# A four-layer kernel on one core: where the next batch's keys stand among a batch's queries, and a second expert product that leaves its result transposed

## The reference, cut to what matters

```python
x = ln(x + linear_attention(x))      # (4, 2048, 256): per head phi = (exp(x orf / d^.25 - norm) + 1e-6) / sqrt(m)
                                     #   kv = sum over l of phi_k v;  out = phi_q kv / (phi_q ksum), then Wo, bo
x = ln(x + fp4_ffn(x))               # gate, up, down with blockwise FP4 values of inputs and weights
x = ln(x + softmax_attention(x))     # 16 heads, rope over the head axis, 2048 x 2048 per head
# experts: 2 groups of 4096 rows, 8 experts, 160 slots each, the best 2 experts of a row
gate, idx = top_k(softmax(x @ w_router), 2)
pos = cumsum(mask) - 1               # a row's slot in its expert; slots >= 160 are dropped
h = relu(einsum('egch,ehf->egcf', expert_in, wi))       # 160 x 256 -> 160 x 1024 per expert
expert_out = einsum('egcf,efh->egch', h, wo)            # -> 160 x 256
x = ln(x + combine(expert_out, gate))
```

## Time and profile before

| | |
|---|---|
| median of 3 runs | 4830.02 us (4827.56 to 4838.83) |
| the profiled execution's own time | 4828.89 us |
| its span in the profile | 4827.1 us |
| PE busy | 4518.8 us, 94% of the span |
| DVE, ACT, POOL busy | 3535.6, 2783.8, 1025.5 us |
| queries with the next keys, three batches | 98.25 to 727.00 us |
| after the third layer's last product | 4545 to 4827.1 us |

### The profile page before, as it was taken

How to read it: one execution, slowest core, us unless ns; L and a number is a source line. 1 busy time by engine, 2 the same in 40 slices (tenths; PEclk the granted TensorE clock), 3 DMA queues, 4 the chain that set the end, 5 groups by cost and what they waited for, 6 DMA issues and landing times. The chain is left out here.

```text
span 4827.1 us, 65506 instructions
## 1 busy us (share of the span) xinstructions
PE 4518.8 (94%) x25453; PEld 1687.8 (35%) x25456; DVE 3535.6 (73%) x3881; ACT 2783.8 (58%) x5253; POOL 1025.5 (21%) x991
## 2 busy tenths in 40 slices
PE   8988888999997999999999999999999999999895
PEld 4434343666662222222222222222222232222374
DVE  2554446887787777898777888777888988898141
ACT  2222222333332777888777777777777767788511
POOL 2333325344431121000121110112111011000223
PEclk9999999999997999999999999999999999999998
DMA  3000100011211333212333222223222121122323
GB/s 101 29 20 23 57 9 19 9 46 46 83 49 56 110 102 101 63 47 70 101 101 116 66 77 73 83 96 127 63 81 80 52 71 60 70 72 74 105 93 58
DMA packets 233083, 333.24 MB, mean 69 GB/s; under 512 B 37026, under 2 KB 174308, under 8 KB 230724
## 3 DMA queue, kind: packets, MB, share of 16 engines
q1 hardware_dynamic: 229892, 321.19, 20.3%
q0 software_dynamic: 2880, 7.87, 0.9%
HBM read 221.50 MB, written 98.04 MB: 66 GB/s over the span
## 5 line engine op out<-in xcount | busy, mean ns | idle before, releaser
L1555 DVE TENSOR_REDUCE mx<-ps 128x1 f32<-128x1024 f32 x2048 | 2405.8, 1218 | 434.3 <-PE ps L717 431.7
L1307 ACT ACTIVATE Pb<-ps 128x512 f32<-128x512 f32 x4096 | 2201.7, 597 | 498.1 <-PE ps L717 493.8
L717 PE MATMUL ps<-QS,KS 98*128 98x512 bf16 x4096 | 1250.4, 386 | 16.7 <-ACT Pb L1307 5.4
L717 PE MATMUL ps<-Pb,VA 128*32 128x512 f32 x8192 | 1097.9, 608 | 0.1
L717 PE MATMUL ps<-KM,QM 64*128 64x512 bf16 x4096 | 661.0, 390 | 58.0 <-DVE mx L1555 55.9
L717 PEld LDWEIGHTS ps<-QS,KS 98*128 98x128 bf16 x4096 | 261.6, 98 | 1082.6 <-ACT Pb L1307 884.5
L717 PEld LDWEIGHTS ps<-KM,QM 64*128 64x128 bf16 x4096 | 179.4, 93 | 614.3 <-issue 347.8
L1877 POOL CAST mrow<-mres 16x128 bf16<-16x128 f32 x64 | 18.0, 280 | 1347.5 <-ACT mres L1137 1347.5
L717 PEld LDWEIGHTS ps<-Pb,VA 128*32 128x32 f32 x8192 | 161.4, 108 | 399.9 <-issue 398.9
L717 PE MATMUL ps<-wdT,hT 128*128 128x256 f32 (+1 forms) x768 | 195.3, 397 | 19.7 <-DVE X L1540 14.8
L1154 ACT ACTIVATE phi<-phi 128x1024 f32<-128x1024 f32 x64 | 67.6, 1057 | 223.6 <-DVE phi L1429 223.6
(11 more groups left out here) (250 smaller groups left out, 4517.8 us busy)
## 6 DMA issues: line engine op xcount, KB each, us to landing
QM<-qd SPq DMA_DIRECT2D x128, 256.0 KB
KM<-kd SPq DMA_DIRECT2D x128, 256.0 KB
qd<-parts SPq DMA_DIRECT2D x96, 256.0 KB, 2.8
kd<-parts SPq DMA_DIRECT2D x96, 256.0 KB, 2.8
QS<-qd SPq DMA_DIRECT2D x64, 384.0 KB
KS<-kd SPq DMA_DIRECT2D x64, 384.0 KB
vdr<-vst SPq DMA_DIRECT2D x64, 256.0 KB, 2.7
den<-rd SPq DMA_DIRECT2D x64, 256.0 KB
```

What stands on the lines that cost most here:

```text
L717: return eng.matmul(out, a, b, start=start, stop=stop, skip_group_check=skip)
L1307: eng.activation(Pb[(u - 1) % 9], o, ACT.Exp, bias=0.0, scale=0.25).then_inc(act_A, 1)
L1555: eng.tensor_reduce(mx4[qc % 2][:, 4 * i + q, h:h + 1], o, AX, ALU.max).then_inc(dve_D, 1)
```

## The change

- `woven` and the two rates go. `beside_queries` issues each step of the queries, then one step of the weights, then a fixed number of key steps: 2 behind the second `q`, 2 behind `nq`, 1 behind the second `pq` of each half, 2 behind the second `num`, 1 behind the second `o`, and none elsewhere; 9 a chunk, 36 a batch.
- `kv` lags `phi` by two tiles in place of one (one more step at the end of a batch's keys: 36).
- In n = 15 the output stages are issued at `OUT_LAST`; the finish of tiles 48 and later has one blank step in place of three, and two `fo` in one step; `oa` of the last quarter is issued ahead of the background work that is left; `second` is rearranged.
- `ed` takes `wo` as weights (128 x 128) and 160 columns of `h`: the result is transposed, 128 x 320 for both halves. ACT copies it to `yT` (4 experts' room), the new `yt` transposes it back by blocks of 128 slots (PE in bank 5, ACT to one of 6 `er` buffers, SP stores it to `eo`), and `yw` takes the own results from `er` block by block: `yo` and its loads go. `eu` has three banks in place of four.

```diff
 OUT = {0: ("oa",), 5: ("ob", "oc"), 7: ("od",), 10: ("oe",), 12: ("og",)}
-KRATE = 46
-WRATE = 45
+
...
+            yield [("phi", n)] + [("kv", n - 2)] * (n % 16 > 1)
             if ahead:
                 yield ahead[j:j + 1] if j < 3 else ahead[3:]
         if b == 0:
             yield [("rl", 2 * C), ("rl", 2 * C + 1)]
+    yield [("kv", 16 * b + 14)]
     yield [("kv", 16 * b + 15), ("kvs", b)]
...
 
+def beside_queries(plan, b, keys, weights):
+
+    behind = {"q": (0, 2), "nq": (2,), "pq": (0, 1, 0, 1), "num": (0, 2), "o": (0, 1)}
+    for units in queries_order(b, range(4), 0):
+        plan += units + next(weights, [])
+        for name, C in (u[:2] for u in units if u[0] in behind):
+            at = sum(u[:2] == (name, C) for u in plan)
+            for _ in range(behind[name][at - 1]):
+                plan += next(keys, [])
+
+
 def weights_order():
...
-            yield []
-        for j in range(4):
-            yield [("fo", T0 + j)]
+        yield from [[]] * (1 if T0 >= 48 else 3)
+
+        for j in range(0, 4, 2):
+            if T0 >= 48:
+                yield [("fo", T0 + j), ("fo", T0 + j + 1)]
+            else:
+                yield [("fo", T0 + j)]
+                yield [("fo", T0 + j + 1)]
         yield [("st2", T0)]
         yield []
         yield [("ap2", T0)]
...
+
+    came = lambda e: range((160 * e + 127) // 128, (160 * (e + 1) + 127) // 128)
+    done = lambda e: range(160 * e // 128, 160 * (e + 1) // 128)
+
+    def back(e):
+        yield from ([("yt", g, b), ("yw", g, b)] for b in done(e))
+
+    yield from ([("xt", g, b)] for b in came(0))
     for e in range(8):
-        for n in range(3):
-            yield [("eu", g, e, n)]
+        yield [("eu", g, e, 0)]
+        if e > 1:
+            yield from back(e - 2)
+        yield [("eu", g, e, 1)]
+        yield [("eu", g, e, 2)]
         if e < 7:
-            for b in range((160 * (e + 1) + 127) // 128, (160 * (e + 2) + 127) // 128):
-                yield [("xt", g, b)]
+            yield from ([("xt", g, b)] for b in came(e + 1))
         if e:
             yield [("ed", g, e - 1)]
+    yield from back(6)
     yield [("ed", g, 7)]
+    yield from back(7)
 
 
 def final_order(g):
-    yield [("yo", g, 0), ("yo", g, 1)] if g else [("yo", g, 0)]
-    yield [("yw", g, 0), ("gp", g, 0)]
     if g == 0:
-        yield [("yp", g, 0)]
-        yield [("yo", g, 1), ("yn", g, 0), ("ys", g, 0)]
-        yield [("yw", g, 1), ("gp", g, 1)]
-        yield [("yp", g, 1)]
-        yield [("yn", g, 1), ("ys", g, 1)]
+        for f in range(2):
+            yield []
+            yield [("gp", g, f)]
+            yield []
...
-    while True:
-        k = min(range(len(streams)), key=lambda n: at[n])
-        at[k] += 1.0 / streams[k][1]
-        units = next(streams[k][0], None)
-        if units is not None:
-            plan += units
-        elif k == 0:
-            return
 
 
 def make_plan():
...
         k = keys_order(b + 1)
-        woven(plan, (queries_order(b, range(4), 0), 49), (k, KRATE), (w, WRATE))
+        beside_queries(plan, b, k, w)
         together(plan, k)
...
                     background()
                 if n > 11 and st % 2 == 0 and ("ap2", 28) in ready:
                     plan.extend(next(moe, []))
+    plan.extend([("oa", 15, 3)])
     while bg:
         background()
     plan.extend(sum(moe, []))
     plan.append(("phase3",))
 
 
...
             yield [(stage, 15, 3) for stage in stages]
         yield [("fl", 60), ("we", 4)]
         for e in (5, 6):
             yield []
             yield [("we", e)]
-        yield []
-        for T in range(60, 64):
-            yield [("fo", T)]
-        yield [("we", 7), ("st2", 60), ("ap2", 60)]
-        ways = list(route_order(1))
-        yield sum(ways[:3], [])
-        yield ways[3] + ways[4] + [("of", 60)]
-        yield ways[5] + ways[6]
-        yield []
-        yield ways[7] + ways[8]
-        yield []
-        yield ways[9]
-        yield ways[10] + ways[11]
-        yield ways[12]
-        yield from inverse_order(1)
-        yield [("gx", 1, b) for b in range(10)]
+        yield from [[]] * 2
+        yield [("fo", 60), ("fo", 61)]
+        yield [("fo", 62), ("fo", 63)]
+        ways, inverse = list(route_order(1)), list(inverse_order(1))
+        yield [("we", 7), ("st2", 60), ("ap2", 60)] + sum(ways[:7], []) + [("of", 60)]
+        yield from [[]] * 6
+        yield sum(ways[7:], []) + inverse[0] + [("iv", 1, 1)]
+        yield from [[]] * 5
+        for j in range(8):
+            yield [("im", 1, j)] + ([("iv", 1, j + 2)] if j < 6 else [])
+        yield inverse[-1] + [("gx", 1, b) for b in range(10)]
 
     together(plan, experts_order(0), second())
...
+    assert top[0] <= mxr_at, (top[0], mxr_at)
     top[0] = low3
     xr.append(take("xr1", [P, 10, 256]))
     assert top[0] <= hi3 + 1024
     top[0] = hi3 + 1024
-    yown.append(take("yown0", [P, 5, 256]))
+    ypar.append(take("ypar0", [P, 5, 256]))
     assert top[0] <= route_at
     top[0] = mxr_at
-    ypar.append(take("ypar0", [P, 5, 256]))
+    yT = take("yT", [P, 2, 640])
     top[0] = 0
     ypar.append(take("ypar1", [P, 10, 256]))
-    top[0] = 8192
-    yown.append(take("yown1", [P, 10, 256]))
     half = lambda buf, g, f: buf[g][:, 5 * f:5 * f + 5, :] if g else buf[0]
...
-            if x > 4:
-                w.wait_ge(act_eu, x - 4)
-            o = bank((1, 2, 3, 5)[(x - 1) % 4])
+            if x > 3:
+                w.wait_ge(act_eu, x - 3)
+            o = bank(1 + (x - 1) % 3)
             c = 160 * e % 640
...
+            for k in range(2):
                 for f in range(8):
-                    d = mm(bank(4)[0:80, 256 * s:256 * s + 256], h3[e % 2][:, f, 80 * s:80 * s + 80], wo[e][:, f, :], f == 0, f == 7)
+                    d = mm(bank(4)[:, 160 * k:160 * k + 160], wo[e][:, f, k * P:(k + 1) * P], h3[e % 2][:, f, :], f == 0, f == 7)
             d.then_inc(pe_ed, 1)
+
+        def yt(g, b):
+            x = 10 * g + b
+            w.wait_ge(act_ed, 8 * g + (P * b + P - 1) // 160 + 1)
+            w.wait_ge(act_yt, x)
+            c = P * (b % 5)
+            for k in range(2):
+                d = tr(bank(5)[:, P * k:P * k + P], yT[:, k, c:c + P])
+            d.then_inc(pe_yt, 1)
 
         stages = {"k": k, "v": v, "kn": kn, "phi": phi_, "kv": kv, "kvt": kvt, "wt": wt, "q": q, "nq": nq_, "pq": pq, "num": num,
                   "o": o, "phase1": phase1, "fold": fold, "tt": tt, "up": up, "dn": dn, "phase2": phase2, "pt": pt, "pa": pa, "px": px,
                   "pp": pp, "pv": pv, "M": M_, "R1": R1, "S": S, "V": V, "fo": fo,
-                  "r6": r6, "r8": r8, "im": im, "phase3": phase3, "xt": xt, "eu": eu, "ed": ed}
+                  "r6": r6, "r8": r8, "im": im, "phase3": phase3, "xt": xt, "eu": eu, "ed": ed, "yt": yt}
...
+            if x > 3:
+                w.wait_ge(pe_yt, 10 * ((x - 4) // 8) + (160 * ((x - 4) % 8 + 1) - 1) // P + 1)
+            c = 160 * (e % 4)
+            copy(yT[:, :, c:c + 160], bank(4)[:, 0:320].rearrange("p (k t) -> p k t", k=2)).then_inc(act_ed, 1)
+
+        def yt(g, b):
+            x = 10 * g + b
+            w.wait_ge(pe_yt, x + 1)
+            if x > 5:
+                w.wait_ge(st_er[x % 6], 16 * (x // 6))
+                w.wait_ge(dve_mix, mix_at["yw", *divmod(x - 6, 10)])
+            copy(er[:, x % 6, :], bank(5)[:, 0:256]).then_inc(act_yt, 1)
 
         stages = {"k": k, "kn": kn, "phi": phi_, "kvs": kvs, "wa": wa, "xa": xa, "ha": ha, "wt": wt, "q": q, "nq": nq_, "pq": pq,
                   "fold": fold, "tt": tt,
                   "up": up, "ap1": ap1, "phase2b": phase2b, "pt": pt, "pa": pa, "px": px, "pp": pp, "pv": pv, "R1": R1, "S": S,
-                  "c1": c1, "r2": r2, "xt": xt, "eu": eu, "ed": ed}
+                  "c1": c1, "r2": r2, "xt": xt, "eu": eu, "ed": ed, "yt": yt}
         for step in plan:
             if step[0] in stages:
...
-                d = eng.scalar_tensor_tensor(out=z[:, j, :], in0=y[:, j, :], scalar=gt[g][:, 0, 5 * f + j:5 * f + j + 1], in1=z[:, j, :],
-                                             op0=ALU.mult, op1=ALU.add)
-            d.then_inc(dve_mix, 1)
+            w.wait_ge(act_yt, 10 * g + b + 1)
+            eng.scalar_tensor_tensor(out=z, in0=er[:, (10 * g + b) % 6, :], scalar=gt[g][:, 0, b:b + 1], in1=z,
+                                     op0=ALU.mult, op1=ALU.add).then_inc(dve_mix, 1)
 
         def yp(g, f):
             z, y = xr[g][:, 5 * f:5 * f + 5, :], half(ypar, g, f)
-            w.wait_ge(dve_mix, mix_at["yw", g, f])
...
                 w.wait_ge(dve_mix, mix_at["yp", g, 0])
             else:
-                w.wait_ge(pe_V, 1024)
+                w.wait_ge(st_of, 256)
+                w.wait_ge(pe_D, d_of("fo", 63))
             y = half(ypar, g, f)
             for j in range(5):
...
-                w.wait_ge(dve_mix, mix_at["yw", g, 0])
-            else:
-                w.wait_ge(st_of, 256)
-                w.wait_ge(pe_D, d_of("fo", 63))
```

(31 more changed lines are left out.)

45 lines of the change are left out of this document (16 added, 29 removed).

## The result

The changed kernel takes 4814.59 us (median of 13 runs, 4796.35 to 4831.47) against 4834.42 (13 runs, 4827.56 to 4841.93) for the kernel before on the same chip: ratio 0.9957, 95% interval 0.9944 to 0.9970, so some 20.8 us less. That is outside the range on record (4753 to 4810). The profiled run took 4804.21 us (span 4802.4). A later series gave 0.9973 (0.9962 to 0.9985); one of its executions took 10585 us and is left out.

What follows compares the result with a forecast made beforehand. PE, busy 94% of the span, was taken to bound the kernel. First attention's 10 us and the experts' 36 summed to 46 off 4828.9, giving 4783; own range 4768 to 4797, with B, C and D 4753 to 4810.

Steps and rivals of the forecast that it cites:

- The end of the third layer: Four `fo` move into the loop; experts still start at 4549.9 within 1 us, and a 3.10 us `fo` wait goes.
- First attention: Key steps at fixed places cut waits and clock loss: 5.2 us a batch, 15.6 for three, net 10 won.
- 6 for the weights: First attention: weight steps directly behind query steps wait for the reciprocal and quantizing on DVE, 6 us more.
- The place behind `nq`: First attention: PE waits there because DVE takes the two key steps' work only behind the norms' four instructions.
- the four fillings: Key-step pairs behind `nq` in four chunks: waits of 2.6, 1.8, 2.9 (4.8 with POOL's addition) and 2.6 us.
- The experts: Transposed `ed` takes 4.34 us, not 6.91, saving 41.1 over 16 experts; with `yt`, waits and end, 36.2 us won.
- the 0.78: Experts' group 1: an amount subtracted beside 0.6 us added for waits, in the sum giving 83.5 us.
- A: First attention: DVE's queue takes back what fillers give, 55 us more lost over twelve chunks, 4848 us; chance 0.04.
- B: First attention: POOL work locks out the norms' DVE casts in all twelve chunks, 17 us, 4800 us; chance 0.08.
- C: Experts: `yt`'s copy waits behind `eu`'s and `ed`'s on in-order ACT, 16 us, 4799 us; chance 0.10.
- D: First attention: the clock holds, its 46 us loss falling to 10, about 30 more won, 4753 us; chance 0.10.

Runs made afterwards that it cites:

- weights_later: Changed kernel with the weight loads of experts 0 to 2 issued twelve steps later: ratio 0.9957 to the kernel before (0.9942 to 0.9972), 4813.89 us.
- early_from_q1: Changed kernel with the output stages of the last sixteenth's first quarter at their old places: ratio 0.9958 to the kernel before, 4812.68 us.
- og_before_r2: `early_from_q1` with `og` issued beside `oe`, so its `aTb` load precedes `R2`'s loads on SP: ratio 0.9934 to the kernel before (0.9920 to 0.9948).
- early_outputs_only: Kernel before with only the last sixteenth's earlier output stages and paired `fo`: ratio 1.0012 (1.0003 to 1.0021), 6 us more.
- key_between_q: Changed kernel with the last sixteenth's old output stages, and one key step moved between a chunk's two `q`: ratio 0.9933 to the kernel before.
- first_only: Kernel before with only the first attention's new order and the later `kv`: ratio 0.9992 (0.9983 to 1.0001), 4 us less.
- experts_only: Kernel before with only the experts' transposed product, the new order behind the last quarter and the new end: ratio 0.9951, 24 us less.
- fo60_later: Changed kernel with the last sixteenth's old output stages, and four more empty steps ahead of the `fo` of T60: ratio 0.9953 to the kernel before, median 4807.90 us.

## Why the prediction was wrong

**The step that failed: "The end of the third layer".** It said that the experts start where they do now "within 1 us", since the four `fo` only move. They started 10.2 us later in the profiled run, though 5.4 us had been won ahead of them. I priced the `fo` as PE work, and that was right (about 3.3 us inside for 3.9 behind). What I put at nothing were the stages that move with them, in all four quarters and not only the last: `oa`, `oc`, `od` and `og` issue DMAs on SP and `ob` waits on DVE's queue, and I had not followed these queues. V's excess is 9.7 to 13.0 us in the traces of six kernels with the old places (15.7 in a seventh) and 26.5 to 32.1 in three traces with the new: some 20 more, 3.3 of it `fo`. Shown by taking each away: 7 to 9 us are `pk` behind the expert weights (`weights_later`, `early_from_q1`), and 9 more went with `og` ahead of `R2` (`og_before_r2`), of which 6 at the two steps of that place and the rest at other steps. What is left, 14 to 15 us, is 4 to 5 over the old, and 3.3 of that are the `fo`. By the timed runs the cost is less, 6 to 9 us; in `early_outputs_only` part of it returned in the tail, as the last quarter's chain got ahead of PE.

**First attention: the sign was right at most, the size was not, and the waits went the other way.** 10 us forecast; 4 with an interval that reaches zero alone, 3 and 1 in two pairs of runs that differ by this order. The forecast had PE's waits fall by 4 us (3 x 3.4 less 6 for the weights) and the clock's loss by 5; the waits rose by 12, and what made the changed kernel's first profile look like a gain was 16 us less of clock loss, of which the second profile has 3. The waits before were read well (92.4 us forecast, 90.5 in the view). For the new order I had 3 x 27.4 and 6 for the weights, 88; there are 102.3. Of the 14 missing, 9.5 are the `qT` waits between the two `q`: I had placed fillers against every wait that the old timeline showed, and this one was hardly to be seen there (1.5 us), because a filler stood in it. `key_between_q` puts it right and lands at 94.0. The place behind `nq` was forecast well: 11.6, 8.6 and 9.9 us in the three batches, where the four fillings add up to 9.9, or 11.8 with POOL's addition. Of the other 5 the largest part is DVE's `X`, awaited behind `o` for 7.8 us in three batches, where 0.9 a batch was put and a share of the 6 for the weights; the rest is small and goes both ways. The batches should have taken 213, 207 and 199 us; they took 218, 210 and 198, and the first was beyond the 215 from which I called myself wrong.

**The experts: right in mechanism and in almost every term.** `ed` 4.35 (4.34), group 1 82.5 (83.5, and 82.7 if the 0.78 is taken off as the text says), behind it 45.8 (46.9), group 0 114.1 from a start that was late (111.2); waits of `r6` and `r8` 2.23 and 0.79 (3.0 and 0.9); `tabs` at 4643.18, 15 later than I said, 10 of it the late start. The tail was 34.9 us shorter in the profiled runs (36). But the timed gain of this part alone is 24 (18 to 29). The base was too high: the tail with the old experts is 271.6 us in the second trace of the kernel before and 270.0 in `first_only`, not 277.2, so some 6 of the 36 were this one execution's (among them ACT's late `xT`, 9.5 us of waits there against 5.9); against these two, the 246.6 of `experts_only` is 23 to 25 less, as timed. A sum made afterwards from these measured parts reads 3 or 4 for the first attention, 6 to 9 lost in the third layer, 24 for the experts: 18 to 22, beside the 20.8 measured.

**The rivals.** A: the waits rose by 12 us, and with the clock's loss the sum fell in one profile and rose by 8 in the other, not by 55; it didn't decide. B: DVE's cast of the norms ended 0.27 us behind POOL's addition in nine chunks of twelve, as before, but was held for long (2.33 us, where it takes 0.42 with nothing beside it) in three only, one in four as forecast, and `stk` releases no wait now:

```profile
431.66 2.34 POOL L1793 TENSOR_TENSOR X<-X,bo 128x1024 f32<-128x1024 f32 x1
431.95 2.33 DVE L1482 CAST stk<-sr 32x512 bf16<-32x512 f32 x1
```

C: the waits for `yT` and its copy are 2.1 and 1.7 us in the whole tail; no. D, in part and by luck: one of two traces had the clock's loss of the batches down from 46 to 30 us, the other at 43.

## What to carry to other kernels

When an edit moves a stage, list every instruction that it issues on every queue in every iteration, and read what stands ahead of each there: here one load of 0.63 us in issue cost 7 us of the layer behind six weight loads, and four of 2.46 us together cost 6 behind eight row loads. A filler hides its own worth: before it is taken from a place, ask what the trace would show there without it. And take the base of a sum from more than one profiled execution where a stage's length varies from run to run.

## What the runs showed of the hardware that was not expected

The spread of one kernel's times goes with the granted clock. The 13 runs of the changed kernel go from 4796.35 us at a mean clock of 0.973 to 4831.47 at 0.965, 35 us for 0.008, and the span times 0.008 is 38. In the first attention's batches the same kernel with the same waits (102.3 and 102.0 us) lost 30 us to the clock in one run and 43 in another, by (1 - c) t over the windows, and the last `q` came 10 us apart. A single profile can't tell 10 us in such a stage, though its waits came out the same within 0.3 us.

A clock that fell with a wait need not come back when the wait is over. In `fo60_later` it fell with a wait of 2.80 us and stayed at half for 30.7 us, though PE hardly waited in that time: the products between 4621 and 4652 stand one behind the other, and in the window from 4625 to 4650 PE is busy for all of the 25 us at a granted clock of 0.50. Why it stayed low is not shown.
